# Blank matmuls on TensorE in the first two attention steps of an attention + mixture-of-experts kernel

## What is computed

```
q = (x @ Wq.T + bq)            # 16 batches, 16 heads of 8
k = (x @ Wk.T + bk)
v = (x @ Wv.T + bv)
attn = softmax(q @ k.T / sqrt(8)) * head_mask
x = layernorm(x + (attn @ v) @ Wo.T + bo)
gate = top-2 of softmax(x @ Wr) over 8 experts, renormalised
routed = sum over e of gate[:, e] * (gelu(x @ Wfc[e] + bfc[e]) @ Wproj[e] + bproj[e])
shared = gelu(x @ Wfc_s + bfc_s) @ Wproj_s + bproj_s
out = layernorm(x + shared + routed)
```

## Time and profile before

| | us |
|---|---|
| median of 3 runs | 705.88 (705.46 to 705.98) |
| profiled execution, its time | 704.37 |
| its span | 702.6 |
| PE busy in the span | 559.1 (80%) |
| DVE busy | 403.5 (57%) |
| ACT busy | 293.5 (42%) |
| POOL busy | 285.9 (41%) |

### The profile page before, as it was taken

The page is one execution under the profiler, slowest core; times in us unless marked ns, Lnnn a source line. Parts: engine busy times, 40 slices in busy tenths (PEclk is TensorE's granted clock), DMA queues, the critical chain, the costliest instruction groups (busy, mean ns, idle before and its releaser), DMA issues. The chain is left out here.

```text
span 702.6 us, 14097 instructions
## 1 busy us (share of the span) xinstructions
PE 559.1 (80%) x5002; PEld 303.0 (43%) x5002; DVE 403.5 (57%) x855; ACT 293.5 (42%) x519; POOL 285.9 (41%) x398
## 2 busy tenths in 40 slices
PE   3899999999999999999999616994007999999200
PEld 1323333333333333333332415993005999999200
DVE  3745555554555555554655485773004998898256
ACT  1244444444444444444444154772003555555015
POOL 5220332133213330333112345887730666666556
PEclk9999999999999999999999857998557999999755
DMA  3121222123114222233221041111129111111094
GB/s 79 53 62 51 62 73 75 52 91 97 54 50 108 80 69 58 85 104 91 75 71 40 3 120 35 44 44 46 53 58 265 42 39 41 40 39 37 18 235 125
DMA packets 72392, 50.30 MB, mean 72 GB/s; under 512 B 9450, under 2 KB 64884, under 8 KB 72324
## 3 DMA queue, kind: packets, MB, share of 16 engines
q1 hardware_dynamic: 67780, 40.92, 21.8%
q0 software_dynamic: 4544, 8.47, 3.8%
HBM read 24.96 MB, written 22.95 MB: 68 GB/s over the span
## 5 line engine op out<-in xcount | busy, mean ns | idle before, releaser
L437 DVE TENSOR_REDUCE row_max<-s_ps 128x2 f32<-128x512 f32 x256 | 173.0, 690 | 165.3 <-PE s_ps L531 162.8
L350 ACT ACTIVATE probs<-ring_ps 128x1024 f32<-128x1024 f32 x128 | 131.2, 1025 | 193.8 <-PE ring_ps L547 193.8
L531 PE MATMUL s_ps<-k_stack,q_stack 24*128 24x256 f16 x512 | 147.2, 404 | 3.6 <-DVE row_max L437 1.9
L547 PE MATMUL ring_ps<-q_stack,k_stack 26*128 26x256 f16 x512 | 146.6, 405 | 0.0
L565 PE MATMUL av_ps<-probs,v_aug 128*32 128x256 f32 x1024 | 138.8, 631 | 0.7 <-ACT probs L350 0.7
L1394 ACT ACTIVATE hid_r<-h_ps_r,bias 128x256 f32<-128x256 f32 x156 | 61.2, 475 | 108.5 <-PE h_ps_r L919 108.5
L1322 POOL DMA_INDIRECT results<-gated,dest x78 | 79.2, 1015 | 65.5 <-DVE gated L1423 52.4
L286 POOL TENSOR_SCALAR max_scaled<-row_max 128x16 f32<-128x16 f32 x32 | 6.6, 205 | 241.4 <-DVE row_max L437 241.4
L531 PEld LDWEIGHTS s_ps<-k_stack,q_stack 24*128 24x128 f16 x512 | 38.5, 110 | 144.2 <-DVE row_max L437 102.5
L903 POOL DMA_INDIRECT slots<-rows,slot_at x64 | 71.3, 1114 | 32.0 <-issue 18.9
L931 PE MATMUL y_ps_r<-w,hid_r 128*128 x312 | 58.2, 220 | 0.0
(11 more groups left out here) (169 smaller groups left out, 1040.0 us busy)
## 6 DMA issues: line engine op xcount, KB each, us to landing
slots<-empty_row SPq DMA_DIRECT2D x6, 780.0 KB, 6.6
expert<-results SPq DMA_DIRECT2D x16, 256.0 KB, 5.1
w_or_slots<-slots SPq DMA_DIRECT2D x3, 1040.0 KB, 11.0
q_stack<-q_rows SPq DMA_DIRECT2D x64, 48.0 KB
k_stack<-k_rows SPq DMA_DIRECT2D x64, 48.0 KB
w_or_slots<-in_w_fc SPq DMA_DIRECT2D x9, 256.0 KB, 2.8
w_or_slots<-in_w_proj SPq DMA_DIRECT2D x9, 256.0 KB, 3.2
x_t<-in_x_t SPq DMA_DIRECT2D x16, 128.0 KB, 2.3
```

Of the source, the lines that this page charges most:

```text
L350: nc.scalar.activation(probs[:, n % PROBS], ring(key), ACT.Exp, scale=SCORE_SCALE).then_inc(ring_emptied, 1)
L437: nc.vector.tensor_reduce(row_max[:, h], s1_ps[:, h % 2], AX_X, ALU.max, negate=True).then_inc(max_done, 1)
L531: mm = nc.tensor.matmul(s1_ps[:, h % 2, t], band_of(q_stack, b, h, TERM_ROWS)[:, t * P:(t + 1) * P], band_of(k_stack, b, h, TERM_ROWS), st ...
L547: mm = nc.tensor.matmul(ring(("pair", b.n, p))[:, n % 2, t], band_of(k_stack, b, h, rows)[:, t * P:(t + 1) * P], band_of(q_stack, b, h, ro ...
```

## The change

Three pieces are added; nothing is removed and nothing else is moved.

1. DVE clears a tile `blank` of 128 partitions by 512 float16 values, ahead of its other work.
2. On PE, after `make_bias_sum` in step 0, 20 matmuls multiply a 128x128 piece of `blank` with all 512 columns of it. Their result goes to `s1_ps`, where the scores write over it later.
3. In step 1, two blank matmuls into `av_ps` go ahead of each slot but slot 4 (30 in all). In step 2 there are two in each of slots 1, 2, 3, 5 and 6 (10), and one into `s1_ps` in each of slots 9, 12 and 14 (3). From step 3 on there is none. Together that makes 63 blank matmuls.

```diff
+        blank = sb("blank", [P, 2 * SEQ], F16)
...
+            nc.vector.memset(blank[:], 0.0).then_inc(blank_made, 1)
             nc.vector.memset(k_stack[:], MAX_UNIT).then_inc(k_cleared, 1)
...
+            def keep_clock(to, times):
+
+                for _ in range(times):
+                    nc.tensor.matmul(to, blank[:, 0:P], blank[:], start=True, stop=True)
+
+            av_bank = av_ps[:].rearrange("p r q -> p (r q)")
...
                         if new.n == 0:
                             make_bias_sum()
+                            pe.wait_ge(blank_made, 1)
+                            keep_clock(s1_ps[:, 0].rearrange("p t k -> p (t k)"), 20)
+                    if now.exists() and not last.exists() and (slot not in ((4,) if now.n == 0 else (0, 4)))\
+                            and (now.n == 0 or slot < 7):
+                        pe.wait_ge(bias_made, 1)
+                        keep_clock(av_bank, 2)
...
+                    if slot in (9, 12, 14) and now.exists() and late.exists() and not last.exists():
+                        keep_clock(s1_ps[:, slot % 2].rearrange("p t k -> p (t k)"), 1)
                     for tile in range(TILES):
```

More of the change, by code:

```diff
@@ L158, in build_attention @@
         warmed = sem("warmed")
+        blank_made = sem("blank_made")
         bias_made = sem("bias_made")
```

## The result

The change made the kernel faster, but by far less than forecast: 694.21 us in the median of 4 runs (685.34 to 701.95) against 705.67 before. The runs fall in two groups, 686.71 and 685.34 us on one side and 701.95 and 701.71 on the other; the ratio of 0.9722 (95% interval 0.9698 to 0.9745) is that of the first group alone. The profiled execution took 686.71 us.

What follows compares the result with a forecast made beforehand. PE was taken to bound attention, running at 1.2 GHz. Twelve steps saving 109.2 us, steps 2, 15, 16 and 17 to 18 saving 5.7, 8.6, 8.0 and 7.8, less 2.0 at the start, gave 569 us, range 540 to 640.

Steps and rivals of the forecast that it cites:

- Attention runs at 1.2 GHz, whatever PEclk says: Attention up to about 391 us: read from matmul durations as 1.2 GHz, the recorded 1.00 being a default.
- The start, 2 us: Twenty blanks after the bias: clock rises some 3.8 us after they begin, scores start later, cost 2 us.
- Steps 1 and 2: Step 1 unchanged at 0.73 us a slot; step 2 falls from 19.20 to about 13.5 us, saving 5.7.
- A fast step of 14.0 us: Full attention step at the raised clock: 14.0 us instead of 23.1, bounds 12.5 (PE's own work) and 16.5.
- the 0.9 us for a maximum in slots 5, 9 and 12: Fast step: PE waits some 0.3 us for a maximum in each of these three slots.
- The 1.8 us of DVE's other work: Full step: DVE's busy time besides maxima, added to 16 maxima at 0.60 us to give 11.4 us.
- the same sum: Savings over steps 2 to 18 less 2.0 us at the start: net -137.3 us, giving 569 us.
- I expect it to hold: Clock after the rise: stays up to step 17, with no PE gap above half a us; 80 in 100.
- a stretch of the experts' stage that held at 1.47 us busy: From 534.40 to 537.80 us, PE busy 1.47 of 3.40 us and clock at 1.00, cited for holding.
- falls back: Rival, 12 in 100: clock falls again in attention, 702 us if in step 3, each further fast step worth 9.1 us.
- never rises: Rival, 8 in 100: the blanks do not raise the clock or have no effect, 17.5 us slower, 723 us.

Runs made afterwards that it cites:

- the last version: Eight blanks at the waits with the later clearing of slots, but two blanks instead of one in slots 6, 10, 13, 15: 622.09 us against 705.01.
- eight blanks at the waits: The change plus, from step 3, one blank in slots 0, 5, 6, 9, 10, 12, 13, 15 where PE waits: median 691.7 us against 764.8.
- the later clearing of slots: Eight blanks at the waits, last two slot-clearing DMAs moved behind steps 18, 19; a second kernel adds step 17 blanks: ratios 0.8812, 0.8814 in four of six runs each.

## Why the prediction was wrong, by its steps

- **Attention runs at 1.2 GHz, whatever PEclk says.** Right, and shown twice: by the durations after the rise, and by PEclk itself, which has 5 for the same rows once a first change is recorded.
- **The start, 2 us.** Near: 1.6 us, with two errors that partly cancel. The clock rose after about 5.2 us of blanks and not 3.8, a figure for which I had given no row, so `project_q` starts at 15.69 us and not 15.3. The two projections then take 0.43 us each from start to start, and not 0.6.
- **Steps 1 and 2.** Step 1 was taken as unchanged and is 0.7 us longer, because two blanks and the scores make 0.86 us a slot and not 0.73; step 2 takes 15.2 us, not 13.5.
- **A fast step of 14.0 us.** Too short: 16.12, inside the bounds of 12.5 to 16.5. Two terms are too small. PE is busy 13.42 us, where I had 12.5 of its own work. The 2.7 us of idle time, where I had 0.9 for DVE and 0.4 for ACT, are these waits of the step from 61.36 us on, with us, times and the longest:

```profile
PE misc_ps L606 <- ACT v_aug L375: 0.8, 1, 0.8
PE s_ps L541 <- ACT probs L352: 0.6, 1, 0.6
PE misc_ps L583 <- POOL max_parts L292: 0.6, 1, 0.6
PE av_ps L575 <- ACT probs L352: 0.5, 1, 0.5
PE ring_ps L591 <- ACT probs L352: 0.3, 1, 0.3
```

None of them is for DVE: the 0.9 us for a maximum in slots 5, 9 and 12 did not come. ACT took 2.2 us instead of 0.4, and POOL 0.6 instead of nothing. (The 1.8 us of DVE's other work was a slip, as 12.45 less 16 maxima of 0.69 is 1.4; nothing hangs on it.) At 16.1 us a step the same sum gives about 600 us with the clock held, not 569, by my estimate: 12 x 7.0 for steps 3 to 14, 6.4 and 5.8 for steps 15 and 16, 4.0 for step 2, 7.8 for the end, less 1.6 and 0.7 at the start, 105.7 in all.
- **"I expect it to hold."** This is the step that failed. The clock was lost at 85.7 us, in step 5, and not held to step 17. I wrote that a fast step had nowhere a gap of more than half a us. It has five gaps, three of them above that (0.79, 0.61 and 0.58 us), and the two falls seen first stand behind those of slots 6 and 0. I had compared with a stretch of the experts' stage that held at 1.47 us busy; that one is made of full-height matmuls, and in attention the clock fell after stretches with 2.61 and 2.23 us busy. So busy time was the wrong thing to count. For the rise the blanks on 24 rows show it: as busy as the full ones, they did not raise the clock. For the fall it is argued from them; I had noted the 24 rows in a rival and still counted in busy time. That the loss is what kept the gain small is shown by the last version, which kept the clock up and is 83 us faster than the kernel before. Why one and the same wait is survived in one step or run and not in another stays open.
- **The rival "falls back".** It is what happened. Its price of 702 us for a fall in step 3 meets two runs of 701.95 and 701.71 (without a trace, but with a mean recorded clock of 0.665 and 0.666 against the 0.697 of the profiled one), in part by luck: it stands on a gain of 5.7 less 2, and what was measured is 4.0 less 1.6 and 0.7, which would give 704. A few fast slots of step 3 may be the rest. Each further fast step is worth 7.0 us (23.1 less 16.1), not 9.1. Its 12 in 100 were too few: no run of the change kept the clock to step 16.
- **The rival "never rises", +17.5 us.** It did not happen here; with blanks on 24 rows it cost 12.3 us, and once, without the 20 blanks, 16.3. That nothing behind the 20 could raise the clock was wrong: without them it rose in step 1, at about 18.1 us, from the blanks in the slots.

## What to carry to other kernels

Read TensorE's level from the durations of one kind of matmul in two stages, not from the recorded clock before its first change. A raised clock shortens PE's work, and so makes gaps where there were none: sum the waits of the fast loop before you count on it to keep the clock, and put full-height filler matmuls into those waits, where they cost least (eight of them made the step 16.8 us long at the waits and 17.0 behind them). Where the times of one kernel spread by tens of us, look in the profile for the step at which the clock was lost; here a bulk DMA in the way of a small one was enough to cause it. And compare two versions for how often they lose it on the same chip, with enough runs.

## What the runs showed of the hardware that I had not expected

- Matmuls on 24 of 128 rows, two a slot and 20 in a row, kept PE as busy as full ones and left the clock at 1.2 GHz (8.71 us for the 20 against 7.09, and 777.03 us against 764.76).
- PE's busy time in a stretch does not by itself tell a fall from a hold. Of the stretches of 3.4 us shown, the clock was lost behind those with 2.61, 2.23 and 2.20 us busy, in a mixture of scores and full matmuls, and held behind one with 2.42 us at the start of step 3 (eight blanks at the waits) and behind one with 1.47 us in the experts' stage. In one and the same kernel the moment differed from run to run (725.5 to 762.5 us).
- The kernel before takes 703 to 706 us on some chips and 763 to 772 on others. A profile of the latter kind (20 blanks only) has PE busy 2.97 us of the 15 from 445 to 460 us, with waits that nothing in the profile explains, where the kernel before on a chip of the former kind has it busy for all 15. Its cause was not looked for.
- Why eight blanks at the waits still lost the clock in four runs of twelve, with the later clearing, stays open: those runs have no trace.
